# A norm step and a low-part step change places in VectorE's order, at the seam of two stages

## The reference

```
x1  = layernorm(x + attention(x))            # 16 heads, latent width 32, rotary, causal
z   = layernorm(x1) * g + b                  # the input of the second layer
S   = z @ slots.T                            # 512 x 1024 logits: 16 experts x 64 slots
D   = softmax(S, over the 512 tokens)        # dispatch
C   = softmax(S, over the 1024 slots)        # combine
out = layernorm(x1 + C @ expert(D.T @ z))    # expert: gelu(a Wg) * (a Wu) @ Wd
```

## Time and profile before

| | |
|---|---|
| median of 3 runs | 1183.93 us (1183.51 to 1184.21) |
| profiled execution | 1186.27 us, span 1184.6 us |
| TensorE (PE) | busy 1138.6 us, 96% |
| VectorE (DVE) | 780.8 us, 66% |
| ScalarE (ACT) | 670.7 us, 57% |
| GpSimd (POOL) | 571.1 us, 48% |
| chain that ended last | PE 81%, DVE 9%, ACT 5% |
| mean granted clock of TensorE | 0.986 |

### The profile page before, as it was taken

How to read it: one execution, slowest core, us unless ns; L and a number is a source line. 1 busy time by engine, 2 the same in 40 slices (tenths; PEclk the granted TensorE clock), 3 DMA queues, 4 the chain that set the end, 5 groups by cost and what they waited for, 6 DMA issues and landing times.

```text
span 1184.6 us, 19139 instructions
## 1 busy us (share of the span) xinstructions
PE 1138.6 (96%) x6882; PEld 903.8 (76%) x6882; DVE 780.8 (66%) x1257; ACT 670.7 (57%) x948; POOL 571.1 (48%) x395
## 2 busy tenths in 40 slices
PE   8799999999999999988899999989999999999996
PEld 5566767676767767656788888878888888888885
DVE  6878787969697978755677777785545454523334
ACT  2556466566656565646787777766555555530112
POOL 5556555655656555512666666645444444430000
PEclk9899999999999999989899999999999999999999
DMA  4645444645565464630044335358555545365761
GB/s 144 153 102 136 118 121 107 161 112 156 124 161 127 119 167 94 178 90 34 25 159 159 124 124 187 107 179 276 158 168 186 163 143 166 108 218 177 243 219 54
DMA packets 127198, 170.23 MB, mean 144 GB/s; under 512 B 47313, under 2 KB 77970, under 8 KB 127122
## 3 DMA queue, kind: packets, MB, share of 16 engines
q1 hardware_dynamic: 124546, 167.88, 48.6%
q10 hardware_dynamic: 2576, 1.35, 0.5%
HBM read 72.13 MB, written 37.75 MB: 93 GB/s over the span
## 4 chain that ended last, share of the span: by engine, by line
PE 81%; DVE 9%; ACT 5%; issue 1%; ACTq 1%; POOL 1%; SPq 1%; DMA 1%; DVEq 0%; POOLq 0%
PE ring L463 12%; PE ring L465 11%; PE ring L464 11%; PE ring L1684 7%; PE tail L1539 6%; PE ring L1528 5%; PE ring L1512 4%; PE tail L463 4%; PE tail L464 4%; PE tail L465 4%; ACT pt L898 3%; PE ring L1561 2%; PE tail L1684 2%; PE tail L1499 2%; PE ring L1615 1%; DVE mx L1206 1%
## 5 line engine op out<-in xcount | busy, mean ns | idle before, releaser
L1206 DVE TENSOR_REDUCE mx<-ring 128x4 f32<-128x512 f32 (+2 forms) x192 | 199.8, 1043 | 74.0 <-PE ring L1515 73.5
L898 ACT ACTIVATE pt<-ring 128x1024 f32<-128x1024 f32 (+1 forms) x192 | 169.0, 881 | 92.3 <-PE ring L1528 88.4
L743 POOL TENSOR_SCALAR_AFFINE_SELECT pt<-pt 128x512 f32<-128x512 f32 x128 | 81.3, 636 | 188.7 <-ACT pt L898 188.7
L1528 PE MATMUL ring<-qks 98*128 98x256 f32 (+3 forms) x512 | 137.0, 371 | 3.5 <-DVE mx L1206 2.0
L1512 PE MATMUL ring<-qks 96*128 96x384 f32 (+3 forms) x512 | 120.5, 338 | 5.5 <-DMA qks<-stg 4.6
L786 POOL TENSOR_TENSOR hl<-hid,hh 128x512 fp32r<-128x512 f32 x64 | 82.6, 1302 | 77.6 <-ACT hh L1015 77.6
L760 POOL TENSOR_TENSOR dl<-e,dh 128x1024 fp32r<-128x1024 f32 x28 | 67.2, 2410 | 84.9 <-ACT e L969 84.9
L1528 PEld LDWEIGHTS ring<-qks 98*128 98x128 f32 x512 | 79.6, 192 | 32.1 <-issue 20.4
L1340 DVE SCALAR_TENSOR_TENSOR hid<-ring,bias_e,gate 128x512 f32<-128x512 f32 x64 | 47.9, 748 | 75.5 <-ACT gate L1009 43.9
L1512 PEld LDWEIGHTS ring<-qks 96*128 96x128 f32 x512 | 80.8, 193 | 21.2 <-issue 6.4
L729 POOL TENSOR_TENSOR rope<-rope,rot 128x1024 f32<-128x1024 f32 x31 | 75.1, 2422 | 36.5 <-DVE rope L1196 36.5
(11 more groups left out here) (254 smaller groups left out, 3098.0 us busy)
## 6 DMA issues: line engine op xcount, KB each, us to landing
qks<-stg SPq DMA_DIRECT2D x378, 128.0 KB, 2.5
c_dram<-c2s SPq DMA_DIRECT2D x32, 512.0 KB, 5.0
c<-c_dram SPq DMA_DIRECT2D x32, 512.0 KB, 6.1
sl_dram<-sls SPq DMA_DIRECT2D x32, 256.0 KB, 3.4
wg<-in_wg SPq DMA_DIRECT2D x16, 512.0 KB, 5.6
wu<-in_wu SPq DMA_DIRECT2D x16, 512.0 KB, 6.5
wd<-in_wd SPq DMA_DIRECT2D x16, 512.0 KB, 7.2
eo<-est SPq DMA_DIRECT2D x32, 256.0 KB, 3.8
```

The lines of the kernel that those rows point to most:

```text
L743: nc.gpsimd.affine_select(out=m, in_=m, compare_op=ALU.is_ge, fill=0.0, base=0, pattern=[[0, GH], [1, P]], channel_multiplier=-1).then_inc ...
L898: nc.scalar.activation(pt[j][:, h:h + heads, 0:n], heads_of(tile, heads, n), ACT.Exp, scale=SCALE).then_inc(empty, 1)
L1206: nc.vector.tensor_reduce(out=mx[:, g, h:h + heads, i], in_=heads_of(tile, heads, (i + 1) * P), axis=AX.X, op=ALU.max).then_inc(empty, 1)
L1528: last = nc.tensor.matmul(scores[:, h, :], qks[0:KS_ROWS + 2, g, 1, h0 + h, j * P:(j + 1) * P], qks[0:KS_ROWS + 2, g, 0, h0 + h, j * P:T], ...
```

## The change

The low part `xn`(b+1) goes from behind the second subtraction to behind the first, in the template of every batch but the last. `DVE_JOIN` grows by nine ones: the last attention step of VectorE, which is `ln`(7), is put down only once the list of numbers has run out, and that is behind `s1`(1,0). Nothing else changes its place; the other engines keep their orders.

```diff
 DVE_FRONT = (
-    ("sumT", -1, 1), ("topT", 0), ("zT", 1), ("sub", 0, 0), ("sub", 0, 1), ("xn", 1), ("sub", 0, 2), ("sub", 0, 3), ("slots", -1, 1),
+    ("sumT", -1, 1), ("topT", 0), ("zT", 1), ("sub", 0, 0), ("xn", 1), ("sub", 0, 1), ("sub", 0, 2), ("sub", 0, 3), ("slots", -1, 1),
     ("s1", 1, 0), ("s1", 1, 1), ("sumT", 0, 0), ("s1", 1, 2), ("s1", 1, 3), ("rows", 1), ("slots", 0, 0),
 )
...
-DVE_JOIN = (5, 4, 4, 3, 2, 2)
+DVE_JOIN = (5, 4, 4, 3, 2, 2, 1, 1, 1, 1, 1, 1, 1, 1, 1)
```

## The result

| | before | after |
|---|---|---|
| median, 7 runs each | 1183.93 us (1183.34 to 1185.59) | 1188.77 us (1187.32 to 1192.59) |
| ratio of the runs, 95% interval | | 1.0045 [1.0033, 1.0057] |
| span of the profiled execution | 1184.6 us | 1187.0 us |
| TensorE / VectorE busy | 96% / 66% | 96% / 67% |

The change makes the kernel slower, by 5.3 us after the ratio (3.9 to 6.7). In the trace the loss has one place. First TensorE's timeline at the seam, the counterpart of the earlier trace rows; its transposes of c2(0,1) are issued at 553.95 now, 4.58 us sooner than in the profile of before, which is not of the change (told further down), so read every time here against that one.

The account below looks back on a forecast made before the run. TensorE, busy 96% of the span, was taken as the bound; sumB(0,0) 6.15 us late plus 1.8 us of clock gave 7.9 us, moving the median from 1183.93 to 1191.8 us, range 1187.5 to 1195.5.

Parts of the forecast that it names:

- likeliest case: The forecast itself, slower at 1191.8 us, with its own range of 1190 to 1194 and a chance of 0.73.
- lost to the clock: At the seam, TensorE comes back from its idle time at 1.2 GHz: 1.8 us lost, at least 0, at most 5.1.
- Leaving the front: At the seam, with ln(7) gone from ahead of rows(0), sumT(0,0) starts at 572.4, 4.9 us sooner than 577.30.
- The margin for a clock that falls at `s1`(1,0): Ahead of sumT(0,0), a low clock costing 1.8 us is covered by 1.9 us spent waiting for GpSimd.
- Entering behind `s1`(1,0): On VectorE, ln(7) beside busy GpSimd: seven small instructions through at seven operations, six left at 0.20 us, free at 584.7.
- Who waits: At the seam, s1(1,1) is reduced late and holds the ring slot, so TensorE starts sumB(0,0) 6.15 us late.
- The other six swaps: In the other batches, xn moved between sub 0 and sub 1 costs 0; at most one subtraction of 1.13 us later.
- Rival 1: In ln(7) at the seam, small instructions hold their place or meet no GpSimd operation; 4.9 us kept, 1179.0; chance 0.12.
- Rival 2: In ln(7) at the seam, three small instructions pass at each end of a GpSimd operation: 1186.8 us; chance 0.05.
- Rival 4: The change doesn't reach the seam, something else sets topT, and both parts cancel near 1184; chance 0.02.
- Rival 3: At the seam the clock stays low, costing 5.1 instead of 1.8: 11.2 us, 1195.2; chance 0.08.

Follow-up runs that it names:

- e4: The changed kernel with ln(7) four places further back, behind s1(1,3) and ahead of rows(1): 1180.52 us, ratio 0.9967 against the kernel before.
- e1: The changed kernel once more, no edit: 1190.55 us, ratio 1.0051 against the kernel before.
- e3: The kernel before with only the move of ln(7) behind s1(1,0), the old order of the subtractions kept: 1190.80 us, ratio 1.0064.
- e5: The changed kernel with ln(7) in two, its 13 small instructions moved behind s1(1,3): 1178.81 us, ratio 0.9967 against the kernel before.

## Why the prediction was right

The forecast was 1191.8 us (range 1187.5 to 1195.5), slower with 0.85. The measured 1188.77 lies in the range, below the likeliest case's own 1190 to 1194 and 3.0 us under its value; the later medians of the changed kernel, 1190.55 and 1190.08 (one run), lie inside. By its own steps, with times given behind the start of c2(0,1), since its absolute times carry the 4.58 us:

| step | forecast | after |
|---|---|---|
| sub(0,0) | 2.0 | 1.94 |
| `s1`(1,0) on TensorE | 4.5 | 4.44 |
| `sumT`(0,0), released by GpSimd's sum | 13.9 | 13.90 |
| first small instruction of `ln` ready | 10.8 | 10.59 |
| instructions held by GpSimd | 7 | 7 |
| GpSimd's chain at its end | 24.9 | 24.44 |
| VectorE free of `ln` | 26.2 | 25.2 |
| `sumB`(0,0) | 30.9 | 29.74 |
| lost to the clock | 1.8 | 1.97 |
| loss at the end of the seam | 7.9 | 6.99 |

- *Leaving the front* was right to 0.1 us, the release by GpSimd included; e4 shows that these 4.9 us can be kept, less what `ln` costs at its new place. The margin for a clock that falls at `s1`(1,0) was right too: e1 used it.
- *Entering behind `s1`(1,0)* was right in mechanism, count and end. The term is 1.0 us too large: the 0.3 us for instructions slipping in between cost GpSimd nothing, and I let only one instruction through at each end, where two more passed: L1244 along with L1243, which it does not wait for (in e3 at an end without a gap), and L1081 in the gap between L767 and L769. So four were left for the free run, not six.
- *Who waits* was right: the tile of `s1`(1,1), by way of ScalarE, at `sumB`(0,0).
- *The other six swaps* at zero: the part from c2(1,2) on is 582.0 us in either kernel and contains five of them; the sixth lies just ahead of it, where TensorE had no wait.
- *Rival 1*, a chain that holds its place once it is through, is refuted by seven operations in a row that each held one. Its argument, that in eight batches only L1243 waited, was not quite right either: in batch 6 L1078 took 0.51 us (517.95 to 518.46), beside a GpSimd mask that ran to 518.43 and had nothing queued behind it. The row that decided against the rival was the pair of `negmax` at 125 us, the only place cited where GpSimd had a second operation queued.
- *Rival 2*, three at each end, falls by the same rows: at the ends without a gap one passed. *Rival 4* falls too: `topT` is reduced at 552.25, ahead of c2(0,1).
- *Rival 3*: the clock was low for 10.2 us (577.5 to 587.7), as before, but 6.2 of them fell into the wait.

What the prediction did not have was the scatter ahead of the seam. It anchored its sum to one profiled execution and took the offset to the median, 2.3 us, for a constant; the forecast for a median over executions is 7.9 whichever that offset is, and the trace's 7.1 stands against medians that moved by 5.3 (3.9 to 6.7), 6.0 (4.4 to 7.8, e1) and 7.6 (5.9 to 9.2, e3). The first of these intervals ends just under 7.1. With a front that varies by 4.6 us, seven runs a side can leave such a gap. Taken together, the 14 executions of the changed kernel and the 48 comparable ones of before differ by 6.5 us in the mean; from their scatter I estimate 5.5 to 7.4, which holds 7.1. That the front is all of the rest was not shown.

## What to carry to other kernels

A step that goes off the critical path goes beside other work, and its price must be taken from rows where it meets that work: `ln` cost 4.3 us with GpSimd idle and 16.5 with GpSimd busy, at the same instructions. A chain of tiny dependent VectorE instructions is expensive beside a full GpSimd queue, since each may pay a whole operation of the other engine; the `bn_` group and the reductions of one operand cost there what they cost elsewhere. Two more things help: look for the place where the other engine has just run dry (here 3.9 us gained instead of 5.3 lost), and compare traces between marks instead of by span, as the parts outside the change have a scatter of their own.

## What the runs showed of the hardware

- In these runs the exclusion has one loser. VectorE's 0.17 us stretched to as much as 2.32 us, while GpSimd's chain was no longer with seven of them in between (19.16 us) than without (19.27). The Trainium skill (SBUF — State Buffer, "Who interferes with whom") says that whichever comes first holds the ports for its instruction. The trace agrees: GpSimd's operation had started 0.05 to 0.57 us ahead of each of the seven that were held. At its end the waiting one passes, and GpSimd's next, which is queued, is there again before the one that depends on it (570.00 against 570.12).
- Which instructions are caught here: small tensor_scalar on SBUF (L1243, L1078) and those with two SBUF operands (L1080 to L1082, L1247). Which are not: `bn_stats`, `bn_aggr` (1.40 and 0.38 us in e5), and the subtractions and maxima that read an operand from PSUM (in before two of L1296 took 2.35 us at 564.55 with GpSimd idle and 2.35 at 567.95 beside it; L1264 and L1274 took 1.23 and 1.21 at 577.50 and 578.64 beside it).
- The granted clock returned to 1.00 at 587.7, 4.1 us after TensorE had resumed at 583.69; before, it took 3.8 us (568.18 to 572.0).
